# Operand parts of the first layer: from SBUF to SBUF in 24 small transfers a sequence, in place of a way through DRAM in ten

## What is computed

```
xn = layernorm(x);  x = x + attention0(xn) + ffn0(xn)     # 16 heads of 8 dims; gated FFN, hidden 384
xn = layernorm(x);  x = x + attention1(xn) + experts(xn)  # block-masked attention; 8 experts, top 2
scores = q @ k.T / sqrt(8);  p = softmax(scores);  o = p @ v   # per sequence and head, 512 x 512
```

## Time and profile before

| | |
|---|---|
| median of 3 runs | 523.88 us |
| the profiled execution | 523.32 us |
| its span, first to last instruction | 521.1 us |
| mean granted clock of TensorE, share of full speed | 0.957 |
| TensorE busy with matmuls | 454.9 us, 87% |
| VectorE busy | 396.2 us, 76% |
| ScalarE busy | 331.9 us, 64% |
| GpSimd busy | 266.5 us, 51% |
| DMA packets and bytes | 140734, 48.27 MB |

### The profile page before, as it was taken

One profiled execution on the slowest core, in us unless ns is written; L12 is line 12 of the kernel. 1 busy time (PEld: TensorE's weight loads), 2 busy tenths in 40 slices (PEclk: granted clock), 3 DMA queues, 4 the chain that ended last, 5 costly groups with the idle time before them and its releaser, 6 DMA issues.

```text
span 521.1 us, 9480 instructions
## 1 busy us (share of the span) xinstructions
PE 454.9 (87%) x3442; PEld 177.3 (34%) x3442; DVE 396.2 (76%) x554; ACT 331.9 (64%) x439; POOL 266.5 (51%) x503
## 2 busy tenths in 40 slices
PE   3555989999999999999999988987999999999962
PEld 1201223324432443243424222221245453555512
DVE  3499889996999699969996988888886777723304
ACT  2301677776677677757776777767766657577570
POOL 6782085724535473787388758874202233163434
PEclk9855899999999999999999999999999999999995
DMA  3797439534820361636162636355721111010025
GB/s 86 223 237 109 75 115 269 152 147 150 175 87 20 124 62 20 64 124 87 20 67 81 119 40 64 120 92 70 97 55 36 42 54 50 2 48 20 31 82 189
DMA packets 140734, 48.27 MB, mean 93 GB/s; under 512 B 109954, under 2 KB 135058, under 8 KB 139858
## 3 DMA queue, kind: packets, MB, share of 16 engines
q1 hardware_dynamic: 138386, 42.93, 39.3%
q0 software_dynamic: 2304, 4.76, 2.7%
HBM read 22.81 MB, written 23.14 MB: 88 GB/s over the span
## 4 chain that ended last, share of the span: by engine, by line
PE 59%; DVE 17%; ACT 9%; issue 8%; DMA 3%; POOL 2%; SPq 1%; ACTq 0%; DVEq 0%; POOLq 0%
PE ps L808 16%; DVE mx L1194 11%; PE ps L792 10%; PE ps L777 8%; ACT PT L1034 6%; PE ps L849 3%; PE ps L735 3%; PE ps L857 3%; PE ps L832 3%; PE ps L850 2%; PE ps L872 2%; PE ps L833 2%; PE ps L869 2%; PE ps L816 1%; POOL y_tokens L550 1%
## 5 line engine op out<-in xcount | busy, mean ns | idle before, releaser
L1194 DVE TENSOR_REDUCE mx<-ps 128x2 f32<-128x1024 f32 x256 | 307.6, 1220 | 57.6 <-PE ps L777 54.2
L1034 ACT ACTIVATE PT<-ps 128x1024 f32<-128x1024 f32 x256 | 258.6, 1025 | 107.6 <-PE ps L792 101.7
L808 PE MATMUL ps<-PT,Vp 128*32 128x512 f32 x1024 | 137.9, 608 | 4.5 <-ACT PT L1034 4.4
L777 PE MATMUL ps<-KO,QO 48*128 48x512 bf16 (+1 forms) x512 | 103.9, 403 | 32.1 <-ACT PT L1034 15.9
L792 PE MATMUL ps<-QO,KO 59*128 59x512 bf16 x512 | 99.9, 388 | 1.3 <-DVE mx L1194 1.1
L550 POOL DMA_INDIRECT y_tokens<-expert_io,meta x40 | 38.4, 961 | 67.5 <-ACT expert_io L1069 50.2
L792 PEld LDWEIGHTS ps<-QO,KO 59*128 59x128 bf16 x512 | 24.5, 93 | 137.2 <-issue 74.9
L1216 DVE SCALAR_TENSOR_TENSOR th<-th,ps 128x320 f32<-128x320 f32 (+1 forms) x56 | 25.5, 455 | 31.9 <-ACT th L1054 31.6
L777 PEld LDWEIGHTS ps<-KO,QO 48*128 48x128 bf16 (+1 forms) x512 | 25.6, 96 | 61.7 <-ACT PT L1034 28.8
L538 POOL DMA_INDIRECT x_places<-xe,place_i x32 | 31.8, 993 | 20.0 <-ACT PT L1034 14.4
L587 POOL CAST mp<-mx 128x32 bf16<-128x32 f32 x16 | 3.4, 211 | 71.9 <-DVE mx L1194 67.9
(11 more groups left out here) (168 smaller groups left out, 491.3 us busy)
## 6 DMA issues: line engine op xcount, KB each, us to landing
z<-part SPq DMA_DIRECT2D x16, 384.0 KB, 2.6
z<-part SPq DMA_DIRECT2D x16, 256.0 KB, 3.0
QO<-z SPq DMA_DIRECT2D x64, 48.0 KB, 2.7
KO<-z SPq DMA_DIRECT2D x64, 48.0 KB, 2.6
x_places<-expert_io SPq DMA_DIRECT2D x2, 1300.0 KB, 7.2
expert_io<-x_places SPq DMA_DIRECT2D x8, 320.0 KB, 3.7
QO<-z SPq DMA_DIRECT2D x6, 384.0 KB
KO<-z SPq DMA_DIRECT2D x6, 384.0 KB
```

Of the source, the lines that this page charges most:

```text
L777: mm = pe.matmul(ps[:, 2 * pair + half, :], rows_of(QO[u % 3], half, 2 * s + jj, rows, (qt, qt + 1)), rows_of(KO[u % 3], half, 2 * s + jj, ...
L808: last = pe.matmul(ps[32 * g:32 * g + 32, PV_BANK, :], Vp[u % 2][:, k, head(s, g), :], PT[:, (2 * t + g % 2) % 4, g // 2, :], start=(s % 2 ...
L1034: act.activation(PT[:, e % 4], ps[:, 2 * pair:2 * pair + 2, :], ACT.Exp).then_inc(exp_done, 1)
L1194: dve.tensor_reduce(mx[:, a, qt, col:col + 5:4], ps[:, 2 * pair:2 * pair + 2, :], AX_X, ALU.max, negate=True).then_inc(max_read, 1)
```

## The change

In layer 0 the parts go from `part` straight to `QO` and `KO`: one transfer for each side, slot and half, 24 a unit, each from 64 partitions of `part` (1 KB a partition) to 8 partitions of the operand tile (8 heads of 1 KB a partition), 64 KB. To make that a plain reordering the weights are permuted so that a row of `part` is 64 * half + 8 * dim + head. For unit 0 ScalarE issues the 8 transfers of the middle parts, SP the other 16. All 24 count on one semaphore, for which TensorE waits at a unit's first maximum pair; `parts` of the next unit waits for the same count in place of `z_written`. The `value_bias` matmul moves ahead of the transposes of unit 1. Layer 1 stays as it is, its DRAM counts beginning at its own first unit.

```diff
@@ -276,7 +275,7 @@
 
         def reads_of(u):
 
-            return 16 * sum(4 if layer(v) == 0 else 16 for v in range(u % 3, u + 1, 3))
+            return 16 * sum(24 if layer(v) == 0 else 16 for v in range(u % 3, u + 1, 3))
 
         def late_reads_of(u):
 
...
@@ -406,14 +405,23 @@
                 sp.wait_ge(unit_done, U)
             sp.dma_start(out[b].rearrange("(t p) d -> p t d", p=P), out_tile(B + b)[:]).then_inc(stored, 16)
 
+        def operand_moves(eng, p, side, i):
+
+
+            if p >= 3:
+
+                eng.wait_ge(exp_done, 32 * (p - 2))
+            eng.wait_ge(part_ready[side], 3 * p + i + 1)
+            for slot in range(*SLOTS[i][side]):
+                for half in range(2):
+                    lo = 64 * half + 8 * slot
+                    eng.dma_start((QO, KO)[side][p % 3][lo:lo + 8], part[i][64 * half:64 * half + 64, side, :]).then_inc(
+                        qk_rows[p % 3], 16)
+
         def operand_writes(sp, p, side):
-            if p >= 2 and side == 0:
+            if p >= B + 2 and side == 0:
                 sp.wait_ge(qk_rows[(p - 2) % 3], reads_of(p - 2))
-                if layer(p - 2) == 1:
-                    sp.wait_ge(late_rows[(p - 2) % 3], late_reads_of(p - 2))
-                if p == 2:
-                    for landed in first_rows:
-                        sp.wait_ge(landed, 16 * 4)
+                sp.wait_ge(late_rows[(p - 2) % 3], late_reads_of(p - 2))
             for i in range(3):
                 sp.wait_ge(part_ready[side], 3 * p + i + 1)
                 a, z, step = SLOTS[i][side]
...
@@ -422,32 +430,11 @@
                 sp.dma_start(dst, part[i][:, side, :].unsqueeze(1).to_broadcast([P, n, S])).then_inc(
                     z_written[side], 16)
 
-        def operand_reads_0(sp, p):
-            if p >= 3:
-                sp.wait_ge(exp_done, 32 * (p - 2))
-            for half in range(2):
-                for side, t in ((0, QO), (1, KO)):
-                    if half == 0:
-                        sp.wait_ge(z_written[side], 16 * Z_WRITES * (p + 1))
-                    src = z_dram[p % 2][side].rearrange("s (d h) t -> (s d) h t", h=H)
-                    sp.dma_start(t[p % 3][64 * half:64 * half + PROD_ROWS],
-                                 src[:, 8 * half:8 * half + 8, :]).then_inc(qk_rows[p % 3], 16)
-
-        def first_reads(sp):
-
-            for side, a, n, landed in ((0, 0, 2, first_rows[0]), (0, 2, 2, first_rows[1]), (1, 0, 2, first_rows[0]),
-                                       (1, 2, 2, first_rows[1]), (0, 4, 4, qk_rows[0]), (1, 4, 4, qk_rows[0])):
-                sp.wait_ge(z_written[side], 16 * Z_WRITES)
-                src = z_dram[0][side].rearrange("s (d h) t -> (s d) h t", h=H)
-                for half in range(2):
-                    sp.dma_start((QO, KO)[side][0][64 * half:64 * half + PROD_ROWS, a:a + n],
-                                 src[:, 8 * half + a:8 * half + a + n, :]).then_inc(landed, 16)
-
         def operand_reads_1(sp, p, a):
 
             if a == 0:
                 for side in range(2):
-                    sp.wait_ge(z_written[side], 16 * Z_WRITES * (p + 1))
+                    sp.wait_ge(z_written[side], 16 * Z_WRITES * (p - B + 1))
                 sp.wait_ge(exp_done, 32 * (p - 2))
             for j in range(4 * a, 4 * a + 4):
                 for half in range(2):
...
@@ -480,14 +467,16 @@
                     load_places(sp, e)
             max_rows(sp, u, 1)
             if p < U:
-                operand_writes(sp, p, 0)
-                operand_writes(sp, p, 1)
+                for side in range(2):
+                    if layer(p) == 1:
+                        operand_writes(sp, p, side)
+                    else:
+                        for i in range(3):
+                            operand_moves(sp, p, side, i)
                 if u < 2:
                     for dst, src in expert_loads[0:2] if u == 0 else expert_loads[2:3]:
                         sp.dma_start(dst, src).then_inc(experts_loaded, 16)
-                if layer(p) == 0:
-                    operand_reads_0(sp, p)
-                else:
+                if layer(p) == 1:
                     operand_reads_1(sp, p, 0)
             if u == U - 2:
                 for e in range(4, 7):
...
@@ -555,8 +544,10 @@
             base, k = 3 * p, 2 * p + side
             f = qk_f[:, side, :]
             eng.wait_ge(qk_f_ready, k + 1)
-            if p >= 1:
-                eng.wait_ge(z_written[side], 16 * Z_WRITES * p)
+            if 1 <= p <= B:
+                eng.wait_ge(qk_rows[(p - 1) % 3], reads_of(p - 1))
+            elif p > B:
+                eng.wait_ge(z_written[side], 16 * Z_WRITES * (p - B))
             eng.tensor_copy(part[0][:, side, :], f).then_inc(part_ready[side], 1)
             eng.wait_ge(part_ready[side], base + 1)
             eng.tensor_tensor(f, f, part[0][:, side, :], ALU.subtract).then_inc(rest_ready[side], 1)
...
@@ -759,16 +750,9 @@
             u, m = q // PAIRS_U, q % PAIRS_U
             s, qt, jj = m // 8, m % 8 // 2, m % 2
             if m == 0:
-                if u == 0:
-                    pe.wait_ge(first_rows[0], 16 * 4)
-                else:
-                    pe.wait_ge(qk_rows[u % 3], reads_of(u))
+                pe.wait_ge(qk_rows[u % 3], reads_of(u))
                 if B <= u < B + 3:
                     pe.wait_ge(mask_rows, 32 * (u - B + 1))
-            if q == PAIRS_U // 4:
-                pe.wait_ge(first_rows[1], 16 * 4)
-            if q == PAIRS_U // 2:
-                pe.wait_ge(qk_rows[0], reads_of(0))
             if m == PAIRS_U // 2 and layer(u) == 1:
                 pe.wait_ge(late_rows[u % 3], late_reads_of(u))
             pair = take_pair(pe, "max", q)
...
@@ -1436,15 +1420,15 @@
             load_x(sp, 2)
             for dst, src in proj_loads:
                 sp.dma_start(dst, src).then_inc(proj_loaded, 16)
-            operand_writes(sp, 0, 0)
-            operand_writes(sp, 0, 1)
-            first_reads(sp)
+            for i in (0, 2):
+                for side in range(2):
+                    operand_moves(sp, 0, side, i)
             row_constants(sp, 0)
             for dst, src in ffn_loads:
                 sp.dma_start(dst, src).then_inc(ffn_loaded, 16)
-            operand_writes(sp, 1, 0)
-            operand_writes(sp, 1, 1)
-            operand_reads_0(sp, 1)
+            for side in range(2):
+                for i in range(3):
+                    operand_moves(sp, 1, side, i)
             max_rows(sp, 0, 0)
             row_constants(sp, 1)
             row_constants(sp, 2)
...
@@ -1516,6 +1500,8 @@
             for side in range(2):
                 second_casts(act, side)
             xnT_copy(act, 1, SIDE)
+            for side in range(2):
+                operand_moves(act, 0, side, 1)
             qk_copy(act, 1, 0, SIDE)
             qk_copy(act, 1, 1, SIDE)
             maxima_copy(act, 0, 0)
...
@@ -1531,11 +1517,11 @@
             qk_mm(pe, 0, 0, PV_BANK)
             qk_mm(pe, 0, 1, 4)
             v_mms(pe, 0, 5)
+            value_bias(pe)
             xnT_mms(pe, 1, SIDE)
             qk_mm(pe, 1, 0, SIDE)
             pe.wait_ge(qk_f_ready, 3)
             qk_mm(pe, 1, 1, SIDE)
-            value_bias(pe)
             pe.wait_ge(v_read, 1)
             pe.wait_ge(part_ready[1], 1)
             for q in range(20):
...
@@ -1567,6 +1553,11 @@
         a = np.asarray(a)
         return np.ascontiguousarray(np.swapaxes(a.reshape(16, 8, -1), 0, 1).reshape(a.shape))
 
+    def halves_first(a):
+
+        a = np.asarray(a)
+        return np.ascontiguousarray(np.swapaxes(a.reshape(2, 8, 8, -1), 1, 2).reshape(a.shape))
+
     def heads_grouped(a):
 
         return np.ascontiguousarray(np.swapaxes(T(a).reshape(2, 4, 16, 128), 0, 1).reshape(128, 128))
...
@@ -1579,11 +1570,11 @@
     qkv_w, qkv_b = np.asarray(L0_attn_qkv_w), np.asarray(L0_attn_qkv_b)
     arrays = {
         "x": np.asarray(L0_attn_x),
-        "wq": np.stack([T(dims_first(qkv_w[0:128])), T(dims_first(L1_attn_Wq))]),
-        "wk": np.stack([T(dims_first(qkv_w[128:256])), T(dims_first(L1_attn_Wk))]),
+        "wq": np.stack([T(halves_first(qkv_w[0:128])), T(dims_first(L1_attn_Wq))]),
+        "wk": np.stack([T(halves_first(qkv_w[128:256])), T(dims_first(L1_attn_Wk))]),
         "wv": np.stack([T(qkv_w[256:384]), T(blocks_last(L1_attn_Wv))]),
-        "bq": np.stack([dims_first(qkv_b[0:128]), dims_first(L1_attn_bq)]),
-        "bk": np.stack([dims_first(qkv_b[128:256]), dims_first(L1_attn_bk)]),
+        "bq": np.stack([halves_first(qkv_b[0:128]), dims_first(L1_attn_bq)]),
+        "bk": np.stack([halves_first(qkv_b[128:256]), dims_first(L1_attn_bk)]),
         "bv": np.stack([heads_grouped(np.tile(qkv_b[None, 256:384], (128, 1)))[:, 0], blocks_last(L1_attn_bv)]),
         "wo": np.stack([heads_grouped(L0_attn_proj_w), heads_grouped(L1_attn_Wo)]),
         "bo": np.stack([np.asarray(L0_attn_proj_b), np.asarray(L1_attn_bo)]),
```

(1 more changed line is left out.)

## The result

The changed kernel takes 538.47 us (median of 5 runs, 537.60 to 539.16) against 523.61 beside it: ratio 1.0281, 95% interval 1.0269 to 1.0293. It is 14.9 us slower. The profiled execution took 538.47 us with a span of 536.0, also 14.9 more than the 521.1 of before, so the traces hold the whole difference.

What follows compares the result with a forecast made beforehand. The prediction took the opening as the bound: TensorE and VectorE wait until the first operand rows land. It added +10.1 us for the first pair and +3.4 for `mT`, +13.5 on 523.32: 536.8, said as 537, range 526 to 553.

Steps and rivals of the forecast that it cites:

- I take 0.85 us a transfer: Unit 0's 24 operand transfers at 0.85 us each, landed at 34.5 us, first maximum pair at 34.6, +10.1 us.
- 0.99: Price in us of a 64 KB transfer into 8 partitions: 1.33 reduced by the factor 1.34 for alternating halves.
- 1.33: Upper bound in us for a 64 KB transfer into 8 partitions, from SP's issue spacing on units 1 and 2's row constants.
- the factor 1.34: Gain from alternating tile halves, taken from first reads at 228 GB/s against unit 1's reads at 170.
- What is late next: Unit 0's `mT` queues on SP behind unit 1's 24 transfers, used by 63.8 us against 60.4 due: +3.4 us.
- Issues at 0.75 us: Issue of a transfer into 8 partitions takes 0.75 us, 0.79 with the gap between two issues.
- just free at my price: Units 2 and 3: 20.4 us of issues and two expert loads fit before `mT`, 24.5 us later; 5 to 9 late at 1.33.
- Hidden work: ScalarE's later `qk_copy(1)` is hidden; GpSimd's opening work, 0.3 us late for `split_max`, is covered by three pairs in PSUM: 0.
- Pure serial transfers: Rival 1: transfers run one after another at 1.33 us each, +36.5 us together, 560 us; chance 0.17.
- Issue is the only price: Rival 2: transfers overlap fully at 0.79 us each, +3 to +5 us in all, 526.5 to 529; chance 0.13.
- The hop was worth more than the issues: Rival 3: with issues at 0.43 + 0.04 us, operands land at 21.9, 2.4 us sooner, 521.4 us; chance 0.08.

Runs made afterwards that it cites:

- the last version: One transfer for both halves in layer 0, 16 destination rows 8 apart, 12 a unit, all from SP, against the kernel before the change: 521.28 us, ratio 0.9954.

## Why the prediction was right, and where it was not

I said 537 (526 to 553) and slower; 538.5 came. The mechanism held: the first pair decides, all 24 transfers stand before it, issues plus narrow destinations cost more than the hop through DRAM, and VectorE's chain moves as a block. But two terms were off and nearly cancelled: 3.1 us too little for the first pair and 1.7 for what I had at nothing, against 3.4 too much for `mT`. That the time came within 1.5 us is in part luck.

- **"I take 0.85 us a transfer", +10.1 us: mis-sized.** With its own formula, (37.55 - 1 - 13.1) / 24 = 0.98 us, and +13.2. The 0.99 that I had from 1.33 and the factor 1.34, and then discounted, was near, but by luck. The grounds for the discount (other sources, two queues) were wrong: with all on SP the rate was the same 67 GB/s. And the factor itself had the wrong reason: alternating halves gives nothing (68 GB/s without it), different slots do. The 1.33 was misread too: the row constants move 64 and 88 KB in turn (8 and 11 partitions), and at their own 63 GB/s 64 KB take 1.04 us. That row, without any factor, was the better price.
- **"What is late next", +3.4 us: did not happen.** The failing step is that SP's issues would go at the pace of the transfers once its queue is full. In unit 0 SP issued at 0.60 to 0.70 us with up to 13 us of transfers outstanding, and unit 1's 24 took 15.8 us (38.31 to 54.1), not 20.4. 5.3 us were to spare. The wait exists: it came in the run with unit 0 through DRAM.
- **Issues at 0.75 us: a little high.** 0.60 to 0.71, after a first of 0.84. The rows of `mT` and the mask (0.74) were near, not equal.
- **Units 2 and 3 "just free at my price": almost.** The 1.0 us at unit 1 is, as far as the profile tells, this: operands, then two expert loads, then `mT`, and the queue of transfers, not the issues, was late (SP was free from 104.5). I had put 0 there.
- **Hidden work:** GpSimd's `split_max` came at 56.70, when 16 maxima were read, and cost nothing; ScalarE's `qk_copy(1)` at 22.56 cost nothing. As forecast.
- **Rivals.** Pure serial transfers (560) did not come, since neighbours overlap by 20 to 30%; where I made them meet in the same rows or 32 apart, 24 took 31.2 us, near that rival's 31.9. "Issue is the only price" (526.5 to 529) is what the kernel becomes with spread rows (526.8). The hop was worth more than the issues only with half as many transfers, in the last version.

## What to carry to other kernels

Before a transfer is put into few partitions, look at how its destination rows lie, and not only at its bytes: a move within SBUF into 8 neighbouring rows was slower than a way through DRAM that moved twice the bytes, written from all 128 partitions and read back into 48 at a time. Rows 2 apart gave twice as much, and successive transfers into rows 32 apart went no faster than into the same rows; how many neighbouring rows make one narrow group, the runs alone do not show. Where the order of the rows is free, as in a contraction, spreading them costs nothing and more than doubled the rate. And in an opening on which every engine waits, the number that counts is when the last needed transfer lands, so count transfers and issues up to there.

## What the runs showed of the hardware

- The destination's rows set the rate of a transfer within SBUF: 8 neighbouring rows 67 GB/s (49 to 53 while successive transfers go to the same rows, or to rows 32 apart), 8 rows 2 apart 136 to 143, 6 apart 143 to 157. 16 rows 8 apart over both halves gave 197 to 202, which is the pace of their issues.
- An issue of such a transfer took mostly 0.60 to 0.71 us whether it had 8 or 16 destination rows, against 0.43 for the reads from DRAM.
- SP is not always held by outstanding transfers: 16 transfers and 7 other issues went out with up to 13 us of work ahead of them, while the row constants of units 1 and 2 stretch to one issue in 1.3 us from the fifth on, before and after, and the FFN loads behind unit 0's constants took 0.42 to 0.50 us in the changed kernel and up to 1.28 with spread rows. What differs (they repeat a few source rows) was not tried; it stays open.
- More queues did not help with spread rows: 526.82 us with two, 527.08 with the issues shared more evenly, 527.05 with a third one.
